# Fused cross-attention and expert FFN on one core: half of the probability transposes moved from TensorE to VectorE and the DMA queue, the softmax scaling moved behind the value product

## The reference

```python
q = (layernorm(x) @ w_q); k = (context @ w_k); v = (context @ w_v)   # 16 heads of 64, all float32
sim = einsum('bhid,bhjd->bhij', q, k) * 64 ** -0.5
out = einsum('bhij,bhjd->bhid', softmax(sim, axis=-1), v)
x = x + out @ w_o + b_o
# then layernorm, a router that picks 2 of 8 experts with a capacity of 640 rows each, and the experts' FFN
```

## Time and profile before

| | us |
|---|---|
| median of three runs | 994.92 |
| lowest and highest | 994.92, 996.96 |
| the profiled execution | 993.48 |
| its span in the trace | 991.4 |
| TensorE busy | 964.9 (97%) |
| VectorE busy | 781.9 (79%) |
| ScalarE busy | 622.3 (63%) |
| GpSimd busy | 281.8 (28%) |
| mean DMA rate over the span | 57 GB/s |

### The profile page before, as it was taken

How to read it: one execution, slowest core, us unless ns; L and a number is a source line. 1 busy time by engine, 2 the same in 40 slices (tenths; PEclk the granted TensorE clock), 3 DMA queues, 4 the chain that set the end, 5 groups by cost and what they waited for, 6 DMA issues and landing times.

```text
span 991.4 us, 23339 instructions
## 1 busy us (share of the span) xinstructions
PE 964.9 (97%) x8434; PEld 876.0 (88%) x8434; DVE 781.9 (79%) x2095; ACT 622.3 (63%) x1740; POOL 281.8 (28%) x440
## 2 busy tenths in 40 slices
PE   8899999999999999999999999999899999999995
PEld 7778888888888888888888888888789999999995
DVE  6887778889898988888888988877987766677662
ACT  5777776777767776777777767776734433344420
POOL 5541121313142232313132241302433233321233
PEclk9999999999999999999999999999989999999998
DMA  8440101011010101011010101000242554344522
GB/s 245 133 133 2 33 1 34 23 34 55 2 54 13 36 14 34 13 33 45 2 44 6 33 9 33 17 1 16 87 136 82 134 140 95 73 124 130 137 28 27
DMA packets 49057, 56.77 MB, mean 57 GB/s; under 512 B 5948, under 2 KB 44842, under 8 KB 48816
## 3 DMA queue, kind: packets, MB, share of 16 engines
q1 hardware_dynamic: 40112, 46.30, 15.0%
q0 software_dynamic: 8832, 8.98, 5.6%
HBM read 36.01 MB, written 24.20 MB: 61 GB/s over the span
## 4 chain that ended last, share of the span: by engine, by line
PE 90%; DVE 5%; ACT 2%; DMA 1%; issue 1%; POOL 0%; POOLq 0%; SPq 0%; ACTq 0%; DVEq 0%
PE psum L613 24%; PE psum L710 12%; PE psum L882 11%; PE psum L696 10%; PE psum L680 10%; PE psum L864 10%; PE psum L727 9%; DVE prob L1146 2%; PE psum L838 1%; ACT prob L945 1%; PE psum L625 1%; PE psum L751 1%; PE psum L743 1%; DMA rows<-slot_table 1%; PE psum L805 1%
## 5 line engine op out<-in xcount | busy, mean ns | idle before, releaser
L945 ACT ACTIVATE prob<-psum,negmax 128x256 f32<-128x256 f32 x512 | 239.9, 488 | 88.5 <-DVE negmax L1135 88.5
L895 ACT ACTIVATE probt<-psum 128x512 f32<-128x512 f32 x256 | 158.1, 626 | 57.5 <-PE psum L696 57.5
L1135 DVE TENSOR_REDUCE negmax<-psum 128x2 f32<-128x512 f32 x256 | 159.8, 680 | 27.3 <-PE psum L680 27.1
L1146 DVE TENSOR_SCALAR prob<-prob,invtot 128x256 f32<-128x256 f32 x512 | 170.5, 396 | 4.5
L696 PE MATMUL psum<-ident,prob 128*128 128x128 f32 x1024 | 150.8, 274 | 1.6 <-DVE prob L1146 1.6
L1055 ACT ACTIVATE hid<-psum,b1t 128x640 f32<-128x640 f32 x64 | 50.9, 795 | 129.3 <-PE psum L864 129.3
L696 PEld LDWEIGHTS psum<-ident,prob 128*128 128x128 f32 x1024 | 120.1, 141 | 10.6 <-ACT probt L895 1.8
L710 PE MATMUL psum<-probt,v 128*64 128x256 f32 x1024 | 125.7, 388 | 0.0
L550 POOL DMA_INDIRECT slot_table<-row,picki x64 | 65.1, 1017 | 174.5 <-DVE picki L1307 148.9
L945 ACT ACTIVATION_READ_ACCUMULATOR prob<-psum,negmax 128x1 f32 x512 | 112.8, 220 | 0.0
L589 POOL DMA_INDIRECT out_rows<-y,rowi x40 | 65.1, 1628 | 165.5 <-DVE y L1366 159.5
(11 more groups left out here) (195 smaller groups left out, 2674.5 us busy)
## 6 DMA issues: line engine op xcount, KB each, us to landing
w1r<-in_w SPq DMA_DIRECT2D x8, 1024.0 KB, 7.9
w2r<-in_w SPq DMA_DIRECT2D x8, 1024.0 KB, 10.4
slot_table<-blank SPq DMA_DIRECT2D x8, 662.5 KB, 9.6
rows<-slot_table SPq DMA_DIRECT2D x7, 662.5 KB, 5.2
xin<-in_x SPq DMA_DIRECT2D x16, 256.0 KB, 2.9
out_rows<-x SPq DMA_DIRECT2D x16, 256.0 KB, 3.2
c<-in_ctxt SPq DMA_DIRECT2D x16, 128.0 KB, 3.1
c<-in_ctxt SPq DMA_DIRECT2D x32, 64.0 KB, 2.9
```

The source lines that it names most:

```text
L895: copy = lambda dst, src, **kw: act.activation(dst, src, ACT.Copy, **kw)
L945: last = act.activation(prob[:, m % 2, u, qb, :], psum[:, u, qb * S:(qb + 1) * S], ACT.Exp, bias=negmax[:, m % 2, u, qb:qb + 1], accum_out ...
L1135: dve.tensor_reduce(negmax[:, m % 2, u, :], psum[:, u, :].rearrange("p (q s) -> p q s", q=ST), AX.X, ALU.max, negate=True).then_inc(sem("m ...
L1146: last = dve.tensor_scalar(prob[:, m % 2, u, qb, :], prob[:, m % 2, u, qb, :], invtot[:, m % 2, u, qb:qb + 1], None, ALU.mult)
```

## The change

1. **Transposes.** In periods 6 to 61 (`MOVED`) TensorE turns only heads 2 and 3 of the four. ScalarE writes the exponentials of heads 0 and 1 of such a period in another arrangement (128x2x4x32), VectorE turns each 32 by 32 block in place (**square0, square1**), and SyncE copies the 512 KB of both heads to memory in one transfer (**lift**) and back into `probt` in four transfers of 32 partitions each (**move**), which puts the blocks in their places. The value product reads the moved heads with a strided pattern.
2. **Scaling.** The multiplications before the transposes are gone in all periods. VectorE takes one reciprocal per period into columns 0 to 7 of `invtot` and turns it in 32 by 32 blocks (**inv**); SyncE writes the turned sums to memory (**inv_out**, runs of 128 bytes) and reads them back broadcast over the partitions in two transfers (**inv_in**) into `invrows`, which has one buffer; VectorE multiplies the value product in PSUM by them (**a_norm**) before it is split.
3. **Order.** The list is written anew, engine by engine within a period, and SyncE's stages are in it too. The slot table is cleared in three parts (periods 2, 3 and 4). `xn` and `x2t` share one buffer, which adds two waits, and `ln1` runs later.

```diff
+MOVED = range(6, PERIODS - 2)
+def turned(m): return (2, 3) if m in MOVED else (0, 1, 2, 3)
...
+        out += [("scores", m)] + ([("pv", m - 2)] if m >= 2 else [])
+        out += [("logits", b - 2)] if r == 3 and 2 <= b else []
+        if four: ...
+        else:
+            out += [("q", m + 1), ("turn2", m - 1), ("k", m + 1), ("turn3", m - 1), ("v", m)]
...
+        out += steps("exp0 exp1", m) + [("q_hi", m + 1)] + ([("a_hi", m - 2)] if m >= 2 else [])
...
+            out += [("copy2", m - 1), ("k_hi", m + 1), ("exp2", m), ("copy3", m - 1), ("exp3", m), ("v_sb", m)]
...
+        out += ([("split_lo", 5)] if m == 1 else []) + steps("max2 max3", m) + [("inv", m - 1)]
+        out += [("a_norm", m - 2)] if m >= 2 else []
+        out += [("square0", m)] if m in MOVED else []
+        out += [("q_lo", m + 1)] + ([("a_lo", m - 2)] if m >= 2 else []) + [("k_lo", m + 1)]
+        out += [("square1", m)] if m in MOVED else []
...
+        out += steps("inv_out inv_in", m - 1) + (steps("lift move", m) if m in MOVED else [])
+        out += {2: steps("clear", 0), 3: steps("clear", 1), 4: steps("clear", 2)}.get(m, [])
+        out += [("traffic", b - 2)] if r == 1 and 2 <= b else []
```

```diff
+            def inv_out(m):
+                sp.wait_ge(sem("inv"), m + 1)
+                sp.dma_start(inv_table[m % 2].rearrange("j (a i) -> a j i", a=GROUPS), invturned[:, m % 2, :])\
+                  .then_inc(sem("inv_out"), 16)
+            def inv_in(m):
+                sp.wait_ge(sem("inv_out"), 16 * (m + 1))
+                if m >= 1:
+                    sp.wait_ge(sem("a_norm"), m)
+                for h in range(2):
+                    sp.dma_start(invrows[h * HD:(h + 1) * HD, :, :], inv_table[m % 2][...])...
+            def lift(m):
+                sp.wait_ge(sem("square"), 2 * (m - MOVED[0] + 1))
+                if m - 2 in MOVED:
+                    sp.wait_ge(sem("pv"), m - 1)
+                sp.dma_start(square_table[m % 2], prob_pair(m)).then_inc(sem("lifted"), 16)
+            def move(m):
+                sp.wait_ge(sem("lifted"), 16 * (m - MOVED[0] + 1))
+                sp.wait_ge(sem("pv"), m - 1)
+                for g in range(GROUPS):
+                    sp.dma_start(probt_pair(m)[g * SQ:(g + 1) * SQ, :]..., square_table[m % 2]...[g])\
+                      .then_inc(sem(f"moved{m % 2}"), 16)
```

```diff
             def turn(m, u):
-                pe.wait_ge(sem("norm"), UNITS * m + u + 1)
+                pe.wait_ge(sem("exp"), UNITS * m + u + 1)
...
             def pv(m):
+                if m in MOVED:
+                    pe.wait_ge(sem(f"moved{m % 2}"), 16 * moves_to(m))
...
-            def norm(m, u): ...
+            def a_norm(m):
+                dve.wait_ge(sem("pv"), m + 1)
+                dve.wait_ge(sem("inv_in"), 32 * (m + 1))
+                at = work_bank("pv", m).rearrange("p (c s) -> p c s", c=2)
+                dve.tensor_tensor(at, at, invrows[:, :, :], ALU.mult).then_inc(sem("a_norm"), 1)
+            def square(m, u):
+                dve.wait_ge(sem("exp"), UNITS * m + u + 1)
+                at = prob_pair(m).rearrange("p (g u c) -> p u g c", g=GROUPS, u=2)[:, u]
+                dve.transpose(at, at).then_inc(sem("square"), 1)
```

More of the change, by code:

```diff
@@ L57, with turned, turns_to, moves_to @@
 assert CAP == ET * P and CAP % 2 == 0 and HALF <= 512
+MOVED = range(6, PERIODS - 2)
+SQ = 32
+GROUPS = P // SQ
+def turned(m):
+    return (2, 3) if m in MOVED else (0, 1, 2, 3)
+def turns_to(m, u):
+    return sum(len(turned(i)) for i in range(m)) + sum(h <= u for h in turned(m))
+def moves_to(m):
+    return GROUPS * len(range(MOVED[0] + (m - MOVED[0]) % 2, m + 1, 2))
 def timeline():
@@ L73, in timeline @@
             *steps("max2 max3", 0), ("split_hi", 4), *steps(k, 1), ("exp1", 0), ("split_lo", 4),
-            *steps("exp2 exp3 v v_sb", 0), ("split_hi", 5), *steps(half[0], 0)]
+            *steps("exp2 exp3 v v_sb", 0), ("split_hi", 5)]
     for m in range(1, PERIODS - 2):
         b, r = divmod(m, PER_B)
[L77 to L91, removed]
-        else:
-            out += steps(half[1], m - 1) + (steps("ln1_stats ln1_root", 1) if m == 1 else []) + steps(q, m + 1)
@@ L94, in timeline @@
[L94 to L109, removed]
+        four = len(turned(m - 1)) == 4
+        out += [("scores", m)] + ([("pv", m - 2)] if m >= 2 else [])
+        out += [("logits", b - 2)] if r == 3 and 2 <= b else []
@@ L110, in timeline @@
+        if four:
+            out += [("q", m + 1), ("turn0", m - 1), ("k", m + 1), ("turn1", m - 1), ("v", m), ("turn2", m - 1)]
+        else:
+            out += [("q", m + 1), ("turn2", m - 1), ("k", m + 1), ("turn3", m - 1), ("v", m)]
         if r == (1 if b else 2) and b + 1 < B:
-            out += steps(xt, b + 1)
+            out += [("xt", b + 1)]
+        if r == 2 and 1 <= b:
+            out += [("o", ST * (b - 1))]
         if r == 2 and 2 <= b:
-            out += steps("x2t x2t_sb", b - 2)
@@ L114, in timeline @@
[L114 to L119, removed]
+            out += [("x2t", b - 2)]
         if r == 0 and 2 <= b:
             out += [("o", ST * (b - 2) + 1)]
-        out += steps("turn3 copy3", m - 1)
-        if r == 1 and 3 <= b:
-            out += [("pos", b - 3)]
+        out += [("turn3", m - 1)] if four else []
@@ new lines, in timeline @@
+        out += [("pos", b - 3)] if r == 1 and 3 <= b else []
+        out += steps("exp0 exp1", m) + [("q_hi", m + 1)] + ([("a_hi", m - 2)] if m >= 2 else [])
+        if four:
+            out += [("copy0", m - 1), ("exp2", m), ("k_hi", m + 1), ("copy1", m - 1), ("exp3", m), ("copy2", m - 1),
+                    ("v_sb", m)]
+        else:
+            out += [("copy2", m - 1), ("k_hi", m + 1), ("exp2", m), ("copy3", m - 1), ("exp3", m), ("v_sb", m)]
+        if r == (1 if b else 2) and b + 1 < B:
+            out += [("xt_hi", b + 1)]
@@ new lines, in timeline @@
+        out += [("copy3", m - 1)] if four else []
+        out += [("gate_exp", b - 3)] if r == 0 and 3 <= b else []
+        out += [("x2t_sb", b - 2)] if r == 2 and 2 <= b else []
+        out += steps("max0 max1", m) + ([("x2add", ST * (b - 2) + 1)] if r == 1 and 2 <= b else [])
+        out += ([("split_lo", 5)] if m == 1 else []) + steps("max2 max3", m) + [("inv", m - 1)]
+        out += [("slot", b - 3)] if r == 2 and 3 <= b else []
+        out += [("a_norm", m - 2)] if m >= 2 else []
+        out += [("bias", b - 2)] if r == 3 and 2 <= b else []
@@ L230, in build @@
         row = sb(rest, "row", [3, ST, ROW])
-        x2t = sb(rest, "x2t", [DC, S])
         bo_all = sb(rest, "bo_all", [D])
```

198 lines of the change are left out of this document (129 added, 69 removed).

## The result

The changed kernel takes **1033.1 us** (median of 4 runs, 1031.9 to 1034.0), the kernel before 995.5 beside it: a ratio of 1.0375, interval 1.0357 to 1.0392. It is slower by 3.8% where I forecast 955 us, and lies outside the range.

What follows compares the result with a forecast made beforehand. TensorE was taken as the bound, with SyncE's queue a nearly equal path after the change. Fourteen blocks falling from 44.2 to 42.0 us give 31, plus 5 and 4: 993.5 to 953.5, predicted as 955 us, range 937 to 1005.

Steps and rivals of the forecast that it cites:

- the rivals: TensorE's floor 937 us (0.12), SyncE's queue eating the gain 969 to 991 (0.20), SyncE bound (0.17), strided operand about 1000 (0.05).
- the third rival: SyncE becomes the bound and the kernel is slower: 1036 us at the upper end, about 1013 half way; chance 0.17.
- my walk through a short period: ScalarE's order from the start of the scores: q ends 5.15, k 6.8; about 0.45 us lost once a block at r = 3.
- The first turn lies in the time in which VectorE would wait for the rounding of q, the second behind the last piece that TensorE wants, so I cost both at nothing: VectorE's two 32 by 32 turns a period, priced at 0.68 us each, were to add no delay.
- start and end: Scaling gone outside the steady blocks: 5 us gained at the start (0 to 9), 4 at the end (0 to 5).
- TensorE, 40.7 us a block: Eight heads' transposes fewer a block, 3.52 us off 44.22; the value product's strided read taken as free.
- ScalarE, 0.45 lost at r = 3: Head 3's exponential late for the scores' second half once a block, making TensorE's path 41.2 us; exponentials taken at 0.46 each.
- VectorE's prices: a_norm 0.68 us, each 512-column turn 0.68 (range 0.40 to twice 0.68); 35.5 us busy a block, 41.0 at the upper end.
- SyncE, 9.6 us a cycle and 41.0 a block; 42.0 taken: Lift 4.05, moves 2.05, inv_out 2.4, inv_in 1.1; four cycles plus 2.6 a block; 42.0 is 0.8 above the longer path.
- The port rule: 32 partitions reach half the ports: moves 2.8 us not 1.7, inv_out about 0.5 later, block 43.0, time about 969.
- Chances: Faster 0.70, same 0.04, slower 0.26; the forecast itself (941 to 966 us) 0.46.

Runs made afterwards that it cites:

- e10: Changed kernel with only SyncE's order altered: inverses out between lift and moves, inverses back behind the moves. 991.2 us on chip 10; the same kernel 1034.0 on chip 12.
- e1: Changed kernel with the value product's rounding (a_hi) and rest (a_lo) ahead of q's on ScalarE and VectorE; 975.8 us, repeated at 977.3.
- e9: Changed kernel with e1's order, e7's earlier exponentials and e10's SyncE order together; 948.7 us on chip 10, 978.0 on chip 12.
- e7: On top of e1: ScalarE runs head 2's exponential before k's rounding and head 3's before the last copy; 964.9 us.
- e8: On top of e1: in every moved period SyncE sends the turned inverses to memory a second time and waits for that; 1057.6 us.
- e3: Changed kernel moving heads in period 61 only, other periods transposing all four on TensorE; scaling behind the value product and new order kept. 1050.3 us.

## Why the prediction was wrong

The forecast was 953.5 us for the profiled execution. The changed kernel has no run on a timely chip; the kernel with SyncE's order alone, equal to it on the one chip where both ran, stands for it there. The 78 us between 955 and 1033 are then

- **43 us, late increments.** No step of mine had them, and the trace of the kernel before did not show them: there no increment of TensorE comes more than 0.43 us behind, scatter or not (the result does not name its chip). None of the rivals had them either, and their cause stays open. That my 1036 for the third rival is close to 1033 is chance: that rival was SyncE as the bound, and TensorE in the changed kernel never waited for a moved head.
- **32 us, the block at 44.3 in place of 42.0**, 14 times 2.3. This is the step that failed: the wait of k and v for a bank, which my walk through a short period put at nothing. It has q end at 5.15 and "k at 6.8 (after 0.44 of transposes and 1.19)", so k starts at once; and "at r = 3 the logits push k back by 0.42" counts the logits as time of TensorE only. They also take a place in the ring, so that k wants the value product's bank there, as v does elsewhere, and the new order has `al` behind q's rounding and rest. Before, `al` starts 1.22 us behind the end of the value product (420.00 to 421.22). In the changed kernel it is 3.3 us (407.54 to 410.86):

```profile
408.73 0.70 DVE L1279 STREAM_TRANSPOSE prob<-prob 128x512 f32<-128x512 f32 x1
410.25 0.69 DVE L1244 SCALAR_TENSOR_TENSOR ql<-psum,qh 128x512 fp32r<-128x512 f32 x1 [0.82 <-ACT qh L1002]
410.86 0.68 DVE L1201 TENSOR_TENSOR al<-psum,ah 128x512 fp32r<-128x512 f32 x1
```

  In a block of e10 TensorE waits 1.73 us for it before k at r = 3 and 0.58 before v at r = 2, and 0.65 for head 3's exponential, counted from start to start less the usual 0.12: 3.0 on top of TensorE's work, of which I had 0.45. The sentence "The first turn lies in the time in which VectorE would wait for the rounding of q, the second behind the last piece that TensorE wants, so I cost both at nothing" held for the longer of these waits: at r = 3 VectorE has done the scaling and the first turn by 409.43 and stands idle for 0.82 us until q is rounded. It failed at r = 2, where in e10 VectorE goes from the maxima through the scaling, the first turn and `ql` to `al` without a gap. e1, which changed only the place of `al` and `ah`, took 2.4 us off the block.
- **6.5 us, start and end.** I took 5 and 4. The scores of period 16 start at 179.93 us in place of 183.27, a gain of 3.3, and from period 60 to the end the timely kernel takes 322.5 in place of 321.7, a loss of 0.8.

These make 81.5, 3 more than there is, which is how well 14 equal blocks describe 64 periods.

Step by step:

- *TensorE, 40.7 us a block.* Right to 0.6 us. e9 comes to 41.3 (eleven blocks between 111.09 and 565.02), and the value product has 385 ns (388 before), so the strided read costs nothing.
- *ScalarE, 0.45 lost at r = 3.* Right in kind: TensorE waits 0.65 us there for the exponential of head 3. e7 took most of that wait away. The exponentials in runs of 32 have 484 ns (488 before).
- *VectorE's prices.* A turn 0.698 for my 0.68, a_norm 0.680 (median) for 0.68, and 35.4 us busy in e10's block for 35.5. Right.
- *SyncE, 9.6 us a cycle and 41.0 a block; 42.0 taken.* The size was right (e8 leaves 10.4 a period, 41.6 a block), and it decides nothing in the changed kernel. The lower end of the cycle, put at 8.1, sums to 8.0 with four issues at 0.42, which changes nothing. e7, where the engines' order no longer hides it, has blocks of 42.4. lift landed in 3.2 to 3.6 us (the pages' medians of e9, e10 and e7) for my 4.05; the rows of inverses in 3.0 in the median and 4.16 in e7's chain, which I had not followed to a_norm.
- *The port rule of the Trainium skill*, SBUF — State Buffer, on the DMA port swizzle, would by my estimate have inv_out 0.5 us later, 2.9. In the changed kernel SyncE waited for it 60.9 us in 34 waits, 1.8 each behind its issue of 0.56, so 2.4: my value without the rule. The Trainium skill's DMA: Bandwidth & Descriptors, Anatomy of one DMA, puts a fixed cost of about 2 us on a transfer that GpSimd issues, most of it the receipt of the write. This 16 KB write is SyncE's; its 2.4 us are near that, and no trace here splits them. e9's order pays because such a wait can be put inside another.
- *Chances.* I had 0.26 on slower, 0.17 of it for SyncE as the bound. e8 shows that this bound exists, 1.9 us of transfers a period away, but the changed kernel is slower for another reason: on a timely chip it would be level with the kernel before.

## What to carry to other kernels

Where work is put between a product and the place that frees its bank, follow the bank: who wants it next, how many places on, and what stands ahead of it on each engine of the way. Here the operations fitted into VectorE's idle time, and the place of `al` behind q's rounding still cost TensorE 2.3 us a block; writing the roundings of a ahead of q's gave 2.4 back. And compare variants on one chip, or put the chip's number beside each run before reading a difference: here it moved the same kernel by 43 us while the kernel before stood still within 0.3%. A cost that starts at some point of a run, as the late increments do at the first scatter, can be priced inside that run, block against block.

## What the runs showed of the hardware

On four of six chips TensorE's semaphore increments came late during GpSimd's four indexed transfers: up to 2.8 us behind the product's start in the changed kernel and 3.2 in e3, where 0.3 to 0.4 is usual. The last of them came within some 0.2 us of each other, 5.7 to 6.3 us after the first of the four was issued. The increments of VectorE and ScalarE in the same stretches came within 0.02 us of the end of their instruction. On the other two the same instructions at the same distances were on time. The kernel before, with the same scatter but a DMA share of 0.09 in place of 0.43 to 0.50, runs equally long on both kinds (994.9 to 995.7 and 993.5 to 995.5 us), so it either has no late increment or nothing in it waits for one. e3, with only the small transfers of the inverses beside the scatter, had it too. The kernel before has no trace from a chip known to be late, so it is open what beside the scatter is needed, and why some chips do it.
